# Routed experts on one Trainium2 core: the second indirect store of each tile waits for a rounding on VectorE two tiles later

## What is computed

```
gates = xf @ rW + rb
topk_vals, topk_idx = jax.lax.top_k(gates, TOP_K)          # TOP_K = 2 of 8 experts
...
h = _gelu(jnp.einsum('td,edh->eth', xf, W1) + b1[:, None, :])   # hidden 512
y = jnp.einsum('eth,ehd->etd', h, W2) + b2[:, None, :]
moe = jnp.einsum('te,etd->td', w, y)
...
x = x + jnp.tanh(g_ffn[0]) * (shared + moe)
```

## Time and profile before

| what | value |
|---|---|
| time, three runs | 526.09, 527.5, 529.23 us; median 527.5 |
| span of the profiled execution | 524.9 us (its own device time is not listed apart; the span lies 2.6 us under the median of the runs) |
| PE busy | 415.9 us (79%) |
| DVE busy | 397.8 us (76%) |
| ACT busy | 340.8 us (65%) |
| POOL busy | 315.9 us (60%) |
| line 622, POOL | 78 transfers, 85.0 us busy, 1089 ns each |
| mean granted TensorE clock | 0.955 |

### The profile page before, as it was taken

How to read it: one execution, slowest core, us unless ns; L and a number is a source line. 1 busy time by engine, 2 the same in 40 slices (tenths; PEclk the granted TensorE clock), 3 DMA queues, 4 the chain that set the end, 5 groups by cost and what they waited for, 6 DMA issues and landing times.

```text
span 524.9 us, 13531 instructions
## 1 busy us (share of the span) xinstructions
PE 415.9 (79%) x4611; PEld 297.2 (57%) x4611; DVE 397.8 (76%) x983; ACT 340.8 (65%) x674; POOL 315.9 (60%) x382
## 2 busy tenths in 40 slices
PE   0377979879998989776784989898999989998930
PEld 0245767758776877554341433344878777776720
DVE  7696769868778778987774896494888768886795
ACT  0536857657787877665663876495677567765743
POOL 9151524494987889598876376650466656666550
PEclk9998989899999999988997989999999999999985
DMA  8767863442333534540011011113122222244119
GB/s 226 223 197 202 223 146 80 103 101 75 78 87 84 114 82 142 178 164 17 26 51 45 27 41 41 47 36 81 36 78 77 70 72 86 67 132 138 58 44 280
DMA packets 71753, 53.19 MB, mean 101 GB/s; under 512 B 7473, under 2 KB 63548, under 8 KB 71688
## 3 DMA queue, kind: packets, MB, share of 16 engines
q1 hardware_dynamic: 64608, 42.96, 30.2%
q0 software_dynamic: 4544, 8.44, 4.6%
q10 hardware_dynamic: 2536, 0.94, 0.7%
HBM read 29.38 MB, written 24.33 MB: 102 GB/s over the span
## 4 chain that ended last, share of the span: by engine, by line
PE 25%; DVE 8%; issue 5%; another core or an unknown queue 5%; ACT 4%; POOL 2%; DMA 1%; ACTq 0%; DVEq 0%; POOLq 0%
PE pAtt L1123 9%; PE pE L1111 4%; PE pS L1111 4%; DVE HH L1490 3%; PE pAtt L1061 2%; PE pMix L1101 2%; PE pS L999 2%; ACT H L767 1%; POOL yd L622 1%; PE pE L999 1%; DVE HH L1486 1%; ACT G L803 1%; DMA YY<-yd 1%; DVE t_X L1543 1%
## 5 line engine op out<-in xcount | busy, mean ns | idle before, releaser
L622 POOL DMA_INDIRECT yd<-Y,XR x78 | 85.0, 1089 | 72.5 <-DVE Y L1529 45.4
L1234 DVE TENSOR_REDUCE t_MX<-pS 128x4 f32<-128x512 f32 x128 | 86.4, 682 | 24.0 <-PE pS L861 22.4
L720 ACT ACTIVATE PT<-pE,t_mbias,t_scl 128x512 f32<-128x512 f32 x128 | 97.1, 788 | 6.6 <-PE pE L861 6.4
L597 POOL DMA_INDIRECT xs<-t_STG,t_pos x64 | 64.2, 1002 | 36.5 <-issue 15.4
L1123 PE MATMUL pAtt<-t_W2h,HR 128*128 x624 | 65.3, 219 | 6.8 <-issue 5.5
L803 ACT ACTIVATE G<-pS,t_b1T,t_inv 128x256 f32<-128x256 f32 x78 | 40.0, 569 | 43.6 <-remote 39.3
L1490 DVE SCALAR_TENSOR_TENSOR HH<-H,t_sc,HH 128x512 f16<-128x512 f32 x64 | 48.4, 761 | 21.6 <-ACT HH L772 14.7
L1521 DVE SCALAR_TENSOR_TENSOR HR<-G,t_sc,HR 128x512 f16<-128x512 f32 x78 | 58.6, 751 | 2.8
L1123 PE MATMUL pAtt<-t_W2l,HR 128*128 x312 | 56.4, 219 | 3.4 <-issue 3.4
L1123 PEld LDWEIGHTS pAtt<-t_W2h,HR 128*128 128x128 f16 x624 | 50.0, 97 | 12.6 <-issue 10.9
L861 PE MATMUL pE<-t_Q,t_K 128*128 128x128 f16 x512 | 51.6, 225 | 5.8 <-DMA t_Q<-MPT 4.8
(11 more groups left out here) (276 smaller groups left out, 1044.5 us busy)
## 6 DMA issues: line engine op xcount, KB each, us to landing
xs<-t_padrow SPq DMA_DIRECT2D x10, 516.0 KB, 5.3
XR<-xs SPq DMA_DIRECT2D x39, 129.0 KB
scr<-QKS SPq DMA_DIRECT2D x16, 256.0 KB, 2.2
t_Q<-scr SPq DMA_DIRECT2D x16, 256.0 KB
t_K<-scr SPq DMA_DIRECT2D x32, 128.0 KB
t_STG<-in_W SPq DMA_DIRECT2D x7, 512.0 KB, 6.4
YY<-yd SPq DMA_DIRECT2D x14, 256.0 KB, 5.8
t_X<-in_x SPq DMA_DIRECT2D x4, 512.0 KB, 6.5
```

Source lines behind the costliest of these rows:

```text
L597: g.indirect_dma_start(k.xs, bass.IndirectOffsetOnAxis(ap=pos[:, n:n + 1], axis=0), k.PAY[:, n, :], None).then_inc(h.di[q], 16)
L622: g.indirect_dma_start(k.yd, bass.IndirectOffsetOnAxis(ap=XR[u][:, q, D:ROW], axis=0), Y[u][:, q, :], None, bounds_check=2 * T - 1, oob_is ...
L720: act.activation(PT[:, m % NPT], pE[g % 2][:], ACT.Exp, bias=k.mbias[:, bt:bt + 1], scale=k.scl[:, bt:bt + 1]).then_inc(s.exp, 1)
L1234: v.tensor_reduce(out=MX[:, n % G // 4, m % 2, m // 2::2], in_=pS[n % 2][:], axis=AX_X, op=ALU.max).then_inc(s.max, 1)
```

## The change

One wait is added in GpSimd's loop over the tiles. Before q1 of tile i, GpSimd waits until `r.hi` has reached 2(i+2)+2, which is when VectorE has finished the second rounding of tile i+2. The last two tiles have no such tile, and no wait.

```
                 u = i % N
                 g.wait_ge(r.y, i + 1)
                 for q in range(2):
+                    if q and i + 2 < NTILE:
+                        g.wait_ge(r.hi, 2 * (i + 2) + 2)
                     g.indirect_dma_start(k.yd, bass.IndirectOffsetOnAxis(ap=XR[u][:, q, D:ROW], axis=0), Y[u][:, q, :], None,
                                          bounds_check=2 * T - 1, oob_is_err=False).then_inc(r.st[u], 16)
```

## The result

The change made the kernel slower: 542.96 us (539.68 to 543.5, 4 runs) against 527.88 us (526.09 to 529.23, 4 runs), a ratio of **1.0273**, 95% interval 1.0235 to 1.031. The forecast was 527.8 us with a range of 515 to 536. The profiled execution spans 541.8 us, 16.9 more than before.

What follows compares the result with a forecast made beforehand. No engine was full; twelve halts of unread cause stopped PE, ACT and DVE together, costing DVE 27 us. Covered shifts 0, fulfilled waits 0, end +0.3 on 527.5 gave 527.8 us, range 515 to 536.

Steps and rivals of the forecast that it cites:

- took the halts as given: Routed stage: the twelve joint standstills of PE, ACT and DVE, 2.3 us each for DVE, were assumed to stay unchanged.
- The sum: Whole kernel: twelve covered shifts cost 0, waits already fulfilled cost nothing, the end adds 0.3 us, giving 527.8 us.
- Shift of 0.80 us in the tile after a halt: GpSimd's q1 after each halt waits for the rounding and starts at 414.16 instead of 413.36, twelve times, under cover.
- The whole run of four is 0.1 to 0.4 us late: GpSimd's four back-to-back transfers after the late q1 start 0.1 to 0.4 us later; its 1.91 us idle absorbs this.
- Shift 0.01: The other two tiles of each three-tile repeat: the rounding is done in time, so q1 moves only 0.01 us.
- a loop on GpSimd's own queue: GpSimd's added wait: only q1 and the next q0 queue behind it, so it can't deadlock or serialize further.
- The run drives the halt: Rival, routed stage: POOL's transfer run causes the halt, so each repeat grows by the run's delay, 531.4 us; chance 0.19.
- More halts: Rival, routed stage: earlier or additional halts cost 2.3 us each, three more making +7 us; chance 0.08.
- The halt breaks up: Rival, routed stage: the change removes halts, 514.3 us with half gone; chance 0.27 that the halt shrinks or goes.
- The late q1 holds up DVE: Rival, VectorE: the rounding waits 0.65 us for the late q1, 7.8 us in twelve repeats, 535.6 us; chance 0.05.
- all of them gone, 27 us: Routed stage, extreme of the faster rival: every halt vanishes, saving 27 us, for 500.8 us; no separate chance given.

Runs made afterwards that it cites:

- e1: Kernel before with the routed stage's 78 indirect stores sent as plain stores from SP's queue to fixed rows, output differing: 514.54 us, ratio 0.9775.
- e14: Kernel before plus a 128x512 f32 GpSimd memset ahead of each second transfer, no wait added, on the chip with halts: 519.43 us, ratio 0.9803.
- e4: Kernel before with q1 of tile i waiting for the next tile's Y (r.y at i+2), later than the change's rounding: 528.32 us, ratio 1.0043.
- e9: The change itself against the kernel before, on a third chip, where the kernel before takes 486.33 us without halts: ratio 1.0021.
- e7: Kernel before plus a 128x512 f32 GpSimd memset ahead of each second transfer, on a chip without halts (before 483.9 us): ratio 1.0116.

## Why the prediction was wrong

- **It "took the halts as given"**: this is the step that failed. The sum priced a shift between fixed halts. Two runs on one chip show that they are a result of what GpSimd sends and when: without indirect transfers none (e1), and with pauses between the pairs other ones, short and with nearly every pair, 28.8 us of ScalarE's waits in place of 39.3 (e14). In the changed kernel they came to 56.6 us, 17.3 more than before, which is about the loss (15.1 us between the medians) where the sum had 0.3.
- **Shift of 0.80 us in the tile after a halt:** right, 1.10 us of idle time ahead of tile 2's q1 in place of 0.30.
- **"The whole run of four is 0.1 to 0.4 us late", and GpSimd's idle time takes it up:** wrong. At the next halt the late q1 joined the run, which began at nearly the same time (383.44, 383.29) but one transfer earlier in the tile, over other work of TensorE, and tile 6's gelus came 2 us late.
- **"Shift 0.01" for the two tiles under cover:** this held only while the rounding was ahead of the halt. In the traces the same wait was 3.19 us for tile 4 and over 2 us again and again after it. The text looked for a loop on GpSimd's own queue and found none; by the stretch read above the loop goes over TensorE: transfer, halt, late rounding, late transfer.
- **The rivals.** "The run drives the halt" had the cause, but let the halt grow by the run's delay, 531.4 us. "More halts" had the mechanism, at 0.08 and with three more. Read were two per four tiles where there had been one per three. An estimate by that rhythm is 19.5 in 39 tiles against 13, though it doesn't hold to the end; at 2.3 us each 6.5 more are 15, against the 15.5 between the first and the last `Y`. So the price of a halt fits, and the number was wrong. The rival "The halt breaks up" had seen that the run gets one transfer longer, and gave that no price; in the trace it stays at four and moves. The probability and the range were too small on this side.
- **"The late q1 holds up DVE", 535.6 us:** not what happened. e4 has q1 later still, at 1.0043. Roundings stay at a median of 481 ns in the change, with a longest of 707; the one at 413.11 took 0.68 us, with the transfer of 412.56 around its start. The Trainium skill, "SBUF — State Buffer", section "Who interferes with whom", has whichever of the two comes second blocked until the other is done, if the rounding runs in a two-port mode; by these rows the rounding began inside the transfer, ended 0.25 us after it (413.79, 413.54) and was stretched by 0.2 us. So the trace shows a part of such a wait: after a full one the rounding would end 0.48 us behind the transfer. Four more are like it, one in each repeat (397.13, 429.06, 445.02, 460.97).
- **What a halt's end costs:** "all of them gone, 27 us" is near what another chip shows: where there are none, in e9, `Y` takes 107.3 us for 38 steps, 25.8 less than before.

**What stays open.** That the halts need the indirect transfers (e1), that they get shorter when the runs do (e14), and that the change's loss is halts (its waits) is shown, the first two on one chip. How the change comes to more of them is read from one stretch of its trace, not tested: whether the run that begins one transfer earlier is enough, or whether tile 4's q1 must also wait for a held rounding. The kernel for it, with the wait at tiles i % 3 = 0 and 2 alone, ran four times and each time met a chip without halts. Also open is what in the chip holds the engines up, and why one chip of five does it. The change was first timed on a chip that runs the kernel before in 527.88 us, like the one with halts; whether it was that one isn't known, and on that one the change itself was not timed again.

## What to carry to other kernels

If several engines stop at once for a releaser that the profile can't name, don't take the stops as given: list what ran just before each, and ask of every moved instruction whether it joins or splits that group. And don't take them as gone because their label is: compare when an engine starts with when its input was done. An added wait is cheap only as long as what it waits for lies outside the stall that it feeds; look for the loop over all engines, not on one queue. And time a change of a few per cent on more than one chip: here it was 2.7% slower on one and free on another, and the filler gained 2% on one and lost 1% on two.

## What was not expected of the hardware

- **One chip of five** took 526 us for the kernel before, four took 484 to 487. The difference lies in stretches with indirect transfers: in the trace of the kernel before and in that of e9 the first of GpSimd's scatters of rows started at 244.1 and at 243.2 us, nearly alike, the first `Y` came at 371.2 and at 355.0, and the 39 tiles took 133.1 and 107.3. The 64 scatters ahead of the routed stage are such transfers too, and in the kernel before the shared experts' gelu has waits on a remote update beside them, which e9 has not:

```profile
ACT H L767 <- remote: 17.0, 5, 6.4
```

- **What is held** looks like TensorE's completions: ScalarE stands idle with its recorded matmuls done (1.98 us at 385.14, 1.12 at 402.87 in e14). But TensorE itself also has gaps with no releaser (before 420.47 in the earlier trace rows), so it may not be these alone. The halt ended 0.77 us after a run at the earlier trace rows (420.65, 421.42) and 0.87 us after a pair in e14; in the changed kernel some gelus got through inside a run, as the one at 387.12 before the transfer's end at 387.17.
- **GpSimd's filler is not one price**, and what decides is which engine begins first. The 128x512 memset took 0.56 us in e7 and a mean of 0.746 in e14. In e14 30 of the 39 begin inside a rounding of VectorE and take 0.73 to 0.82 us, as the one at 403.09 inside this:

```profile
402.97 0.48 DVE L1523 TENSOR_SCALAR HR<-G,t_sc 128x512 f16<-128x512 f32 x1
```

The 8 that touch no rounding take 0.57 in the median. In e7 it is the other way round: the rounding begins inside the memset, and the rounding is stretched.
